# Attention in one megakernel: transposed scores in four row tiles at once, maxima subtracted in f32, weighted sums moved behind the next scores

## The reference

```python
qkv = (x @ qkv_w + qkv_b).reshape(b, s, 3, h, hd)          # h = 16 heads, hd = 16
logits = jnp.einsum('bqhd,bkhd->bhqk', q, k)
logits = jnp.where(causal_mask, -jnp.inf, logits) * scale
att = jax.nn.softmax(logits, axis=-1)
out = jnp.einsum('bhqk,bkhd->bqhd', att, v).reshape(b, s, d)
return out @ out_w + out_b
```

## Time and profile before

| | us |
|---|---|
| median of the runs shown | 933.86 |
| the profiled execution | 933.2 |
| its span | 931.3 |
| attention: first scores of the first sequence to first scores of the last | 36.59 to 203.16 |
| TensorE busy, whole span | 741.3 (80%) |
| VectorE / ScalarE / GpSimd busy, whole span | 534.0 / 345.7 / 373.2 |

### The profile page before, as it was taken

One profiled execution on the slowest core, in us unless ns is written; L12 is line 12 of the kernel. 1 busy time (PEld: TensorE's weight loads), 2 busy tenths in 40 slices (PEclk: granted clock), 3 DMA queues, 4 the chain that ended last, 5 costly groups with the idle time before them and its releaser, 6 DMA issues.

```text
span 931.3 us, 12689 instructions
## 1 busy us (share of the span) xinstructions
PE 741.3 (80%) x4032; PEld 502.4 (54%) x4033; DVE 534.0 (57%) x990; ACT 345.7 (37%) x654; POOL 373.2 (40%) x284
## 2 busy tenths in 40 slices
PE   7699999997999679999924476877878687624958
PEld 5577777776655436666613344555445353302548
DVE  1555555554231105443215578888888977985885
ACT  1232232234222122223212364553654653214973
POOL 0122222220065400000068278768768777540535
PEclk9899999997899889999966598799789976656965
DMA  9970000000011261111112220210201202000002
GB/s 261 403 307 0 0 0 0 0 1 1 1 18 31 49 164 46 41 43 40 39 35 47 95 81 1 80 56 25 80 11 70 81 1 80 0 0 1 0 10 70
DMA packets 35366, 52.83 MB, mean 57 GB/s; under 512 B 18101, under 2 KB 30297, under 8 KB 32985
## 3 DMA queue, kind: packets, MB, share of 16 engines
q1 hardware_dynamic: 19977, 48.55, 15.1%
q0 software_dynamic: 15360, 3.92, 2.3%
HBM read 42.66 MB, written 9.59 MB: 56 GB/s over the span
## 4 chain that ended last, share of the span: by engine, by line
PE 50%; POOL 18%; DVE 16%; issue 8%; DMA 4%; ACT 3%; SPq 1%; POOLq 0%; DVEq 0%; ACTq 0%
PE ps L1531 8%; POOL arena L484 6%; PE ps L1543 4%; POOL slots_in L516 4%; DVE arena L1231 4%; POOL xn L525 4%; PE ps L1337 3%; PE ps L1371 3%; PE ps L1637 3%; DVE work L881 3%; PE ps L1703 2%; POOL arena L487 2%; PE ps L1365 2%; DVE arena L1224 2%; PE ps L1667 2%
## 5 line engine op out<-in xcount | busy, mean ns | idle before, releaser
L484 POOL TENSOR_TENSOR arena<-arena 128x904 f32<-128x904 f32 x64 | 125.3, 1958 | 85.8 <-DVE arena L1231 56.6
L1231 DVE TENSOR_TENSOR_SCAN arena<-ps,arena 128x452 f32<-128x452 f32 x128 | 133.6, 1085 | 5.4
L752 ACT ACTIVATE ps<-arena,sh_w 128x448 f32<-128x448 f32 x128 | 80.7, 636 | 134.9 <-DVE arena L1231 134.3
L1703 PE MATMUL ps<-arena,const 128*128 128x452 f32 x128 | 79.9, 713 | 59.9 <-POOL arena L487 59.5
L1531 PE MATMUL ps<-arena,work 128*128 x176 | 85.4, 610 | 0.3 <-issue 0.3
L1224 DVE TENSOR_TENSOR arena<-arena,ps 128x904 f32<-128x904 f32 x64 | 69.3, 1083 | 17.3 <-PE ps L1694 17.1
L426 POOL TENSOR_TENSOR xT<-work 128x452 f32<-128x452 f32 x16 | 15.1, 941 | 155.6 <-DVE work L868 155.6
L487 POOL TENSOR_TENSOR arena<-arena 128x452 f32<-128x452 f32 x64 | 73.1, 1142 | 5.0
L516 POOL DMA_INDIRECT slots_in<-xn,slot x16 | 38.0, 2373 | 73.8 <-issue 73.8
L1703 PEld LDWEIGHTS ps<-arena,const 128*128 128x128 f32 x128 | 23.8, 228 | 75.1 <-POOL arena L487 71.4
L521 POOL MEMSET arena<- 128x464 f32 x1 | 0.5, 484 | 153.1 <-PE ps L1543 153.1
(11 more groups left out here) (244 smaller groups left out, 1520.2 us busy)
## 6 DMA issues: line engine op xcount, KB each, us to landing
arena<-c_rows SPq DMA_DIRECT2D x8, 1808.0 KB, 6.5
arena<-in_ex_w SPq DMA_DIRECT2D x8, 1536.0 KB, 20.9
slots_in<-work SPq DMA_DIRECT2D x1, 2816.0 KB, 18.6
work<-slots_in SPq DMA_DIRECT2D x22, 128.0 KB, 2.1
slots_out<-work SPq DMA_DIRECT2D x22, 128.0 KB, 1.7
out<-resid SPq DMA_DIRECT2D x8, 224.0 KB
arena<-in_patches SPq DMA_DIRECT2D x3, 576.0 KB, 6.1
sh_w<-in_sh_w SPq DMA_DIRECT2D x1, 1536.0 KB, 11.9
```

The lines of the kernel that those rows point to most:

```text
L484: pool.tensor_tensor(read[kp], state[kp], c_all[par][:, 2 * c:2 * c + 2, :].unsqueeze(2).broadcast_to([P, 2, KT, N]), ALU.mult)\
L752: act.activation(decay_ps(n)[:, :, 1:], delta[par].rearrange("p k (b s) -> p (k b) s", b=GB)[:, :, 1:], ACT.Exp, scale=a_neg[:, 2 * c + n: ...
L1231: dve.tensor_tensor_scan(state[kp][:, n].rearrange("p k s -> p (k s)"), decay_ps(n).rearrange("p q s -> p (q s)"), drive[kp][:, n].rearran ...
L1703: pe.matmul(ps[:, 6, 0:KT * N], ident, read[kp][:, 0].rearrange("p k s -> p (k s)"), start=c == 0, stop=False, skip_group_check=True).then ...
```

## The change

- `scores_t` loses its two waits and its halves: all four quads are issued side by side in four row tiles.
- `turn_max` comes ahead of `scores_t` and waits for all four maxima and for the copied sums of b-1 (bank 7). The maxima stay in f32 in columns 32 r to 32 r + 3, so that after the transposition each quad's maxima lie in its own 32 rows; ScalarE copies them once (`nmT`). The bf16 split is gone from ScalarE and VectorE.
- `less_max` is 16 f32 matmuls of 32 rows in four row tiles, head by head.
- `weighted(b-1)` stands behind `scores(b)`; its values are kept in two buffers in turn (`vh[par]`), for which the loops of TensorE and VectorE do two steps in one turn. `scores(b)` waits, quad by quad, for the exponentials of b-1.
- `turn_heads(b-1)` moves behind `scores_t`, `turn_back(b-1)` behind `less_max`, `project(b-1)` behind `values(b+1)`.
- ScalarE does `outputs(b-1)` first in its step; VectorE takes the values ahead of `add_resid`. GpSimd sets a second buffer of ones at the start.

```diff
-        max_pick = pl.take((HEADS * P // 2,), 96).bitcast(BF16).rearrange("p (h m) -> p h m", h=HEADS)
+        max_pick = pl.take((4, S))
...
-        negmax = pl.take((3, 32), S)
-        nm_rest, nm_hi, nm_mid, nm3 = ...
-        vh = pl.take((HEADS, 32), S)
+        negmax = pl.take((QUADS, 32), S)
+        nmT = pl.take((S,))
+        vh = [pl.take((HEADS, 32), S) for _ in range(2)]
...
-            def high_parts(b):
+            def maxima_turned(b):
                 act.wait_ge(nmT_ps, b + 1)
-                for dst, rows in ((nm_hi, 96), (nm3, 32)):
-                    act.activation(dst[0:rows, :], ps[0:rows, 7, 0:S], ACT.Copy).then_inc(nm_hi_ready, 1)
+                act.activation(nmT, ps[:, 7, 0:S], ACT.Copy).then_inc(nm_copied, 1)
...
             def step(b, back=True, more=True):                    # ScalarE
+                if back:
+                    outputs(b - 1)
                 if more:
                     turn_x(b + 1)
-                high_parts(b)
+                maxima_turned(b)
                 if back:
                     turn_back(b - 1)
                 exps(b)
-                outputs(b)
...
-            def step(b, first=False, last=False):                 # VectorE
+            def step(b, par, first=False, last=False):
                 if not last:
                     normalise(b + 1)
                 maxima(b)
                 if not first:
                     weigh(b - 1)
-                split(b)
                 if not last:
                     queries_keys(b + 1)
+                    values(b + 1, 1 - par)
                 if not first:
                     add_resid(b - 1)
-                if not last:
-                    values(b + 1)
...
+            def scores(b, first=False):                           # TensorE
                 pe.wait_ge(kz_ready, b + 1)
                 for t in range(KT):
                     for r in range(QUADS):
+                        if t == 0 and not first:
+                            pe.wait_ge(probs_ready, QUADS * (b - 1) + r + 1)
...
             def scores_t(b):
                 pe.wait_ge(qz_ready, b + 1)
-                for half in range(2):
-                    pe.wait_ge(negmax_ready, 4 * b + 2 * half + 2)
-                    for t in range(KT):
-                        for r in range(2 * half, 2 * half + 2):
+                for t in range(KT):
+                    for r in range(QUADS):
...
-            def turn_max(b):
-                pe.wait_ge(negmax3_ready, b + 1)
+            def turn_max(b, first=False):
+                pe.wait_ge(negmax_ready, QUADS * b + QUADS)
+                if not first:
+                    pe.wait_ge(attn_copied, b)
...
             def less_max(b):
-                pe.wait_ge(nm_hi_ready, 2 * b + 2)
-                pe.wait_ge(nm3_ready, 2 * b + 2)
-                for r in range(QUADS):
-                    for j in range(4):
-                        last = pe.matmul(ps[0:S, 3 + r, j * S:(j + 1) * S], max_pick[:, 4 * r + j, 0:S], nm3, start=False, stop=True, skip_group_check=True)
-                    last.then_inc(scoreT_ps, 1)
+                pe.wait_ge(nm_copied, b + 1)
+                for j in range(4):
+                    for r in range(QUADS):
+                        rows = slice(32 * r, 32 * r + 32)
+                        last = pe.matmul(ps[0:S, 3 + r, j * S:(j + 1) * S], max_pick[rows, j, :], nmT[rows, :], start=False, stop=True,
+                                         tile_position=(32 * r, 0), skip_group_check=True)
+                        if j == 3:
+                            last.then_inc(scoreT_ps, 1)
...
+            def step(b, par, back=True, more=True, first_back=False):    # TensorE, conditions left out
+                scores(b); weighted(b - 1); turn_x(b + 1); turn_max(b); scores_t(b); turn_heads(b - 1)
+                queries_keys(b + 1); less_max(b); turn_back(b - 1); values(b + 1); project(b - 1)
```

More of the change, by code:

```diff
@@ L310, in build @@
         attn_nT_ps, attn_nT_ready = sem("attn_nT_ps"), sem("attn_nT_ready")
-        oproj_ps, resid1_ready, bias_added, negmax3_ready = sem("oproj_ps"), sem("resid1_ready"), sem("bias_added"), sem("negmax3_ready")
-        kz_ready, qz_ready, nm_hi_ready, nm3_ready = (sem("kz_ready"), sem("qz_ready"), sem("nm_hi_ready"),
-                                                                         sem("nm3_ready"))
+        oproj_ps, resid1_ready, bias_added = sem("oproj_ps"), sem("resid1_ready"), sem("bias_added")
+        kz_ready, qz_ready, nm_copied = sem("kz_ready"), sem("qz_ready"), sem("nm_copied")
         out_done = sem("out_done")
@@ L441, in pool_attention @@
             pool.wait_ge(attn_in, ATTN_LOADS * 16)
-            pool.wait_ge(pool_set, 7)
+            pool.wait_ge(pool_set, 8)
             with pool.Fori(0, B) as b:
@@ L507, in _ @@
             pool.memset(negmax, 0.0).then_inc(pool_set, 1)
-            pool.memset(vh, 1.0).then_inc(pool_set, 1)
+            for half in vh:
+                pool.memset(half, 1.0).then_inc(pool_set, 1)
             pool_attention(pool)
@@ L578, in act_attention @@
             step(B - 1, more=False)
+            outputs(B - 1)
             act_rstd(act, 1, BUT_ONE_SEQS)
@@ L869, in queries_keys, with values @@
                                   qk_b.unsqueeze(2).broadcast_to([P, 2 * KT, S]), ALU.add).then_inc(qk_ready, 1)
-            def values(b, first=False):
+            def values(b, par):
                 dve.wait_ge(v_ps, b + 1)
-                if not first:
-                    dve.wait_ge(av_ps, b)
-                dve.tensor_tensor(vh[:, :, 0:HD], ps[0:S, 0, 0:D].rearrange("p (h e) -> p h e", h=HEADS),
+                dve.tensor_tensor(vh[par][:, :, 0:HD], ps[0:S, 0, 0:D].rearrange("p (h e) -> p h e", h=HEADS),
                                   v_b.rearrange("p (h e) -> p h e", h=HEADS), ALU.add).then_inc(v_ready, 1)
@@ L880, in maxima @@
                     dve.wait_ge(score_ps, QUADS * b + r + 1)
-                    dve.tensor_reduce(negmax[:, 0, 4 * r:4 * r + 4].unsqueeze(2), ps[0:S, 3 + r, 0:4 * S].rearrange("p (j s) -> p j s", j=4),
+                    dve.tensor_reduce(negmax[:, r, 0:4].unsqueeze(2), ps[0:S, 3 + r, 0:4 * S].rearrange("p (j s) -> p j s", j=4),
                                       AX.X, ALU.max, negate=True).then_inc(negmax_ready, 1)
[L883 to L895, removed]
             def weigh(b):
@@ L918, in step @@
                     weigh(b - 1)
-                split(b)
                 if not last:
                     queries_keys(b + 1)
+                    values(b + 1, 1 - par)
                 if not first:
                     add_resid(b - 1)
-                if not last:
-                    values(b + 1)
             dve.wait_ge(attn_in, ATTN_LOADS * 16)
             normalise(0, first=True)
-            dve.tensor_copy(max_pick, const[0:96, C_REP:C_REP + HEADS].unsqueeze(2).broadcast_to([96, HEADS, P])).then_inc(pick_done, 1)
+            dve.tensor_copy(max_pick, const[:, C_REP:C_REP + 4].unsqueeze(2).broadcast_to([P, 4, S])).then_inc(pick_done, 1)
             queries_keys(0)
[L931 to L935, removed]
+            values(0, 0)
+            step(0, 0, first=True)
+            with dve.Fori(0, (B - 2) // 2) as i:
+                for half in range(2):
+                    step(2 * i + 1 + half, 1 - half)
+            step(B - 1, 1, last=True)
             dve.wait_ge(stats_done, B + B - 1)
@@ L1054, in dve_clips @@
             dve.wait_ge(clip_exp, 1)
-            q = Seq(dve, f_step, 2 * B)
+            q = Seq(dve, f_step)
             q.step(dve.tensor_scalar(clip_sig[:, :], clip_sig[:, :], 1.0, QMAX, ALU.add, ALU.mult))
@@ L1095, in dve_ffn @@
             dve.wait_ge(xmax_ready, B)
-            q = Seq(dve, f_step, 2 * B + 2)
+            q = Seq(dve, f_step, 2)
             def scales(turn, source, parts, dst):
@@ L1344, in values @@
                 last.then_inc(v_ps, 1)
-            def scores(b):
+            def scores(b, first=False):
                 pe.wait_ge(kz_ready, b + 1)
@@ L1359, in scores_t @@
                 pe.wait_ge(qz_ready, b + 1)
-                for half in range(2):
-                    pe.wait_ge(negmax_ready, 4 * b + 2 * half + 2)
-                    for t in range(KT):
-                        for r in range(2 * half, 2 * half + 2):
-                            rows = slice(32 * r, 32 * r + 32)
-                            pe.matmul(ps[0:S, 3 + r, 2 * t * S:2 * (t + 1) * S], qkT[rows, KT + t, :], qz[rows, t, :, :],
-                                      start=t == 0, stop=False, tile_position=(32 * r, 0), skip_group_check=True)
+                for t in range(KT):
+                    for r in range(QUADS):
+                        rows = slice(32 * r, 32 * r + 32)
+                        pe.matmul(ps[0:S, 3 + r, 2 * t * S:2 * (t + 1) * S], qkT[rows, KT + t, :], qz[rows, t, :, :],
+                                  start=t == 0, stop=False, tile_position=(32 * r, 0), skip_group_check=True)
```

(53 more changed lines are left out.)

4 lines of the change are left out of this document (removed).

## The result

The changed kernel is slower. Eight executions have a median of 942.02 us beside 932.86 for the kernel before; the ratio is 1.0086, 95% interval 1.0056 to 1.0117. That is 6 to 8 us more; 6.4 were forecast. The profiled execution took 943.77 us, its span 942.0.

The account below looks back on a forecast made before the run. TensorE's queue was taken to bound the attention step; with added waits it goes from 11.17 to 11.60 us, +6.45 over fifteen steps, -0.1 in the last, giving 940.3 us; range 931.5 to 945.5.

Parts of the forecast that it names:

- (a): Transposed scores four at once: block falls from 2.02 to 0.96 us, but starts only when all four maxima are there.
- (b): TensorE's wait for VectorE's maxima: some 0.7 us, turned maxima at M+2.78, where M is the first mask's start.
- rival 5: Transposed scores: the four row tiles run two at a time, +1 us a step, 955 us; chance 0.03.
- (c): TensorE blocks from turned maxima through queries and keys, including 0.10 for entering row tiles: done at M+6.99.
- (d): Row-tiled f32 subtraction of the maxima: 1.08 us with its edges, next block at M+8.07; removing the split gains nothing in the loop.
- Rival 2: Row-tiled subtraction: weight loads aren't hidden, rounds of 0.19 instead of 0.097 us, +0.7 a step, 951 us; chance 0.07.
- (e): ScalarE: exponentials follow subtraction, turning back and its copy; they start at M+8.72 and take 1.87 us, to M+10.59.
- (f): Next scores wait for the exponentials until M+10.64, TensorE ready at 10.13, 0.5 us idle; next mask at M+11.60.
- rival 3: No change: the last exponential ends before M+10.13, step 11.09 us, 932.7 to 935 us; chance 0.17.
- (g): Other queues: GpSimd's key spreading in time; VectorE's normalisation done at M+11.89 to 12.12, at worst 0.08 us late.
- rival 1: VectorE's normalisation arrives last, each step takes 11.68 us, +0.51, 941.5 us in all; chance 0.13.
- Rival 4: TensorE's queue alone decides, no exponential waited for, changes of form hidden: step 10.85 us, 929.2 us; chance 0.12.

Follow-up runs that it names:

- b1: Kernel before with only the transposed scores changed, to one wait for all four maxima and four row tiles at once: step 11.18 us, ratio 1.0006.
- e1: Changed kernel with TensorE turning the attention back ahead of the subtraction of the maxima: steps of 11.20 and 11.47 us in turn, mean 11.34.
- e2: Changed kernel with turning back ahead of the subtraction, and projection and VectorE's residual add ahead of the values: every step 11.20 us, ratio 1.0017.
- c1: Changed kernel with bf16 split and quad-by-quad subtraction restored, maxima turned after four-at-once transposed scores, turning back before subtraction, projection before values: step 10.70 us, ratio 0.9931.
- c3: c2 again, timed against the kernel before: median 926.65 us, ratio 0.9925.
- b2: Kernel before with only the row-tiled f32 subtraction, its maxima handling and the split's removal, TensorE's block order kept: step 11.45 us, ratio 1.0063.
- a1: Changed kernel as it is, timed and profiled again beside the kernel before: steps of 11.62 us, first step 12.21, ratio 1.0065.
- c2: As c1, but transposed scores in two halves that wait for two maxima each, as in the kernel before: step 10.68 us.

## Why the prediction was right

Direction, size and cause hold; the step that the forecast rests on was worked out to 11.60 us and measured at 11.62. (The row is the one that a view from 91.7 to 91.9 us gives; what was read from it, second loads 0.09 behind the first, is right.)

- **(a), (b) Four at once, behind the wait.** Said: block 0.96, queue free at M+2.03, turned maxima at M+2.78. Measured from 83.15: the block 0.97 (86.12 to 87.09), turned maxima at M+2.73. The lag behind the last reduction was 0.06, near the lower bound of 0.05, not 0.10. The wait is 0.71 us by the idle time of the weight loads. A block of 0.97 rules out rival 5, row tiles two at a time. b1 shows what lies under it: the gain was never on the path.
- **(c) to (d).** Turned maxima and entering row tiles took 0.24 instead of 0.20, the subtraction 0.99 (90.21 to 91.20) instead of 0.98 and came at M+7.06 instead of 7.09. Rival 2, weight loads not hidden, is out: it needed some 1.7 (0.98 + 0.7).
- **(e), (f) The exponentials.** Said: start at M+8.72, last quad through at M+10.64, 0.5 us of waiting. Measured M+8.76, M+10.67, 0.53. TensorE was ready at M+10.13, as said, and the last exponential ended at M+10.62, so rival 3 is out. e1 takes 0.42 of the wait away in every second step (11.20 instead of 11.62), and 0.28 on average, by nothing but an earlier transpose, so this cause is shown.
- **The changes of form.** The estimate of 0.1 each held roughly: turning back took 0.25 (91.20 to 91.45) where it takes 0.19 among full blocks, and entering the subtraction moved queries and keys from 1.79 to 1.87. Those ahead of one of the two waits are hidden by it. Those between the waits, into the transposed scores, into the subtraction and out of it, stand ahead of the exponentials and are in the 11.62. In e2, with the same number of changes, the step is back at 11.20, so they are not what made the change slower than the kernel before. They are part of why e2 stays 0.5 us above c1. Block by block the two timelines differ by 0.14 for the longer subtraction, 0.09 for entering and 0.04 for leaving it, 0.14 for the maxima turned ahead of the scores and 0.07 for a wait in the scores. That division is read from rows and was not tried piece by piece.
- **(g), rival 1.** VectorE's normalisation ends at 95.12, 0.09 ahead of the reductions, in the changed kernel: not the bound, but next in line. e1 made it the bound in every second step.
- **Rival 4, the faster side.** Its condition was exponentials 0.5 earlier, which the change as written doesn't meet. Its time of 10.85 doesn't follow from the condition either: e2 has them 0.4 earlier, with 0.07 of waiting left, and its step is 11.20. Without that wait it would be 11.13, near the 11.09 of rival 3; the rest of rival 4 was that changes of form would hide. c1 gets to 10.70 by another subtraction.
- **The sum.** 6.4 against 6.9 in the attention (table load at 220.93 instead of 214.05, both from the traces): 14 steps of +0.45, the first with +0.38, 0.16 from a later start of the first step, and nothing gained in the last. There the forecast had -0.1 and was wrong: the exponentials ended at M+8.85, as said, but the sums were copied 0.52 behind that, at M+9.37, instead of 0.4. So part of the closeness is small misses of either sign. The timed ratios give 6.1 and 8.0 us.

## What to carry to other kernels

When a queue is shared by a chain that passes through other engines, work out where each engine's result is needed and how long before it is there, not only how much work the queue holds: here 1.05 us of matmuls were removed beside a reduction, which gave nothing, and two transposes put behind a block instead of ahead of it cost 0.4 us of a step. A wait is worth filling only with work that nobody further on is waiting for. The weighted sums were such work: with them in the wait and the f32 subtraction left out, c3 is 0.7% faster than the kernel before. (They were not moved quite alone; turning the heads made room for them.) A form that delivers all four parts at its end lets the next engine start later than one that delivers them one by one, 1.08 us instead of 0.41; whether that costs anything depends on who waits. In b2 it cost nothing.

## What the runs showed of the hardware

The busy share of TensorE hid a stall. With matmuls of three row tiles in flight while the fourth waited for its operand, the profile counts no idle time for 0.53 us of waiting, and of the 0.71 ahead of the turned maxima it counts 0.49. The weight loads (PEld) show 0.71 for the first, but only 0.17 for the second; its whole size comes from comparing the starts of blocks (1.49 from scores to mask instead of 0.96).

Half-clock stretches move from execution to execution. In a1 the attention's first step held one: granted clock 0.50, that is 1.2 GHz, from 42.1 to 45.3 us, after a stretch at full clock in which TensorE was busy for 4.15 of 6.60 us (columns as in the earlier trace rows). The third row is the first profile of the changed kernel, busy for 4.07 of the same 6.60 us, and it stayed at full clock up to 48.1 us; so the busy time ahead doesn't tell the two apart here:

```profile
35.30:41.90 6.60, 4.15 (x43) 2.58 (x42) 3.62 (x7) 0.63 (x2) 2.62 (x3) 1.00 1.03 434
42.10:45.30 3.20, 3.20 (x14) 2.69 (x12) 0.00 (x0) 0.00 (x0) 0.00 (x0) 0.50 1.01 430
35.30:41.90 6.60, 4.07 (x44) 2.48 (x43) 3.44 (x7) 0.62 (x2) 2.61 (x3) 1.00 1.01 428
```

It cost 12.21 - 10.57 = 1.64 us, a quarter of the 6.4 that were to be measured. c1's profile has one at the same place (first step 11.39 us; c2, at full clock there, 9.64), the first profiles of both kernels have none. What follows the attention varied by 5 us, 716 to 721, for reasons that stay open. The length of a step at full clock agreed within 0.01 us from run to run (11.62 in both profiles of the changed kernel, 10.68 in c2 and c3), so steps can be compared where totals can't.
